# A Mamba block with a mixture of experts: one state product changes engines, a loss correction moves ahead of a projection, and ScalarE's first steps are reordered

## The reference, cut to what matters

```
h  = layernorm(layernorm(x)) @ in_proj_w.T        # 256 -> 512 channels
h  = silu(causal conv of 4 taps over time)
proj = h @ x_proj_w.T                             # 1 dt, 16 B, 16 C values per token
dt = softplus(proj[0] * dt_w + dt_b)
for every channel d and every state n of 16:
    state[t] = exp(-exp(A_log)[d,n] * dt[t,d]) * state[t-1] + B[t,n] * h[t,d]
    y[t,d]  += state[t] * C[t,n]                  # plus D[d] * h[t,d]
x1 = x + layernorm(silu(y) @ out_proj_w.T + layernorm(x))
out = x1 + layernorm(shared expert + one of 8 routed experts of layernorm(x1))
```

## Time and profile before

| | |
|---|---|
| median of three runs | 1394.33 us (1393.41 to 1395.83) |
| the profiled execution: its time / its span | 1393.79 us / 1392.0 us |
| busy of the span: PE, DVE, ACT, POOL | 86%, 77%, 57%, 75% |
| chain that ended last, by engine | PE 59%, DVE 21%, ACT 12%, issue 5% |
| scans (DVE L1126) | 256, the first at 51.0 us, the last at 969.4 us |
| mean granted TensorE clock | 0.968 of full speed |

### The profile page before, as it was taken

How to read it: one execution, slowest core, us unless ns; L and a number is a source line. 1 busy time by engine, 2 the same in 40 slices (tenths; PEclk the granted TensorE clock), 3 DMA queues, 4 the chain that set the end, 5 groups by cost and what they waited for, 6 DMA issues and landing times.

```text
span 1392.0 us, 15477 instructions
## 1 busy us (share of the span) xinstructions
PE 1194.2 (86%) x4894; PEld 535.3 (38%) x4895; DVE 1069.5 (77%) x1409; ACT 796.5 (57%) x1386; POOL 1045.7 (75%) x558
## 2 busy tenths in 40 slices
PE   5668978887996996997798798898999999999995
PEld 2222223222332432432332243243545656656663
DVE  4588899999999999899999998799241116677675
ACT  5757679779778877877967875736431111111111
POOL 0579999999999999899999999989033723554453
PEclk9889999999999999999999999999999999999998
DMA  3921210330340141042034015001278522222220
GB/s 109 277 69 60 94 61 1 122 138 0 103 157 0 63 152 46 14 140 106 1 108 137 0 63 207 20 1 55 82 270 291 180 64 73 86 79 79 84 63 15
DMA packets 72068, 127.67 MB, mean 92 GB/s; under 512 B 8759, under 2 KB 48448, under 8 KB 67904
## 3 DMA queue, kind: packets, MB, share of 16 engines
q1 hardware_dynamic: 60432, 103.72, 22.2%
q0 software_dynamic: 7152, 16.81, 3.8%
q10 hardware_dynamic: 4416, 6.29, 1.3%
HBM read 97.79 MB, written 31.76 MB: 93 GB/s over the span
## 4 chain that ended last, share of the span: by engine, by line
PE 59%; DVE 21%; ACT 12%; issue 5%; DMA 1%; DVEq 0%; POOLq 0%; POOL 0%; ACTq 0%; SPq 0%
DVE state L1126 11%; PE psX L1697 10%; PE psY L1574 10%; PE psX L1632 5%; PE bank L1531 5%; DVE bx L1114 5%; PE bank L1487 4%; ACT psX L793 3%; PE psY L1645 3%; PE bank L1714 2%; PE psY L1714 2%; PE bank L1469 2%; PE bank L1470 2%; PE bank L1471 2%; DMA xin<-in_x 1%
## 5 line engine op out<-in xcount | busy, mean ns | idle before, releaser
L517 POOL TENSOR_TENSOR state<-state,cbc 128x1024 f32<-128x1024 f32 x256 | 599.2, 2367 | 10.2 <-DVE state L1126 10.2
L1126 DVE TENSOR_TENSOR_SCAN state<-psX,bx 128x1024 f32<-128x1024 f32 x256 | 580.9, 2282 | 25.9 <-ACT psX L793 22.2
L793 ACT ACTIVATE psX<-dt,aneg 128x511 f32<-128x511 f32 x512 | 331.3, 680 | 166.4 <-DVE state L1126 166.0
L506 POOL TENSOR_TENSOR bx<-xh,bbc 128x1024 f32<-128x1024 f32 x120 | 284.8, 2374 | 89.3 <-DVE state L1126 47.1
L1574 PE MATMUL psY<-state,ident 64*64 64x512 f32 x2048 | 268.0, 617 | 0.0
L1531 PE MATMUL bank<-prow,ident 128*128 128x512 f32 x272 | 151.0, 638 | 59.4 <-DVE bx L1114 57.5
L1114 DVE TENSOR_TENSOR bx<-xh,bank 128x1024 f32<-128x1024 f32 x136 | 162.9, 1198 | 15.4 <-PE bank L1531 15.3
L998 ACT ACTIVATE sg<-psX 128x512 f32<-128x512 f32 x39 | 23.3, 597 | 196.6 <-PE psX L1697 191.4
L1574 PEld LDWEIGHTS psY<-state,ident 64*64 64x64 f32 x2048 | 61.9, 133 | 166.3 <-issue 118.4
L1531 PEld LDWEIGHTS bank<-prow,ident 128*128 128x128 f32 x272 | 44.7, 192 | 149.5 <-DVE bx L1114 107.8
L581 POOL DMA_INDIRECT ysl<-shared_rows,idx x39 | 40.3, 1034 | 80.7 <-DVE idx L1292 75.7
(11 more groups left out here) (212 smaller groups left out, 1798.2 us busy)
## 6 DMA issues: line engine op xcount, KB each, us to landing
cbc<-bc_rows SPq DMA_DIRECT2D x32, 1024.0 KB, 6.6
bbc<-bc_rows SPq DMA_DIRECT2D x16, 1024.0 KB, 6.4
slot_in<-ao SPq DMA_DIRECT2D x1, 5011.5 KB, 35.2
xsl<-slot_in SPq DMA_DIRECT2D x39, 128.5 KB
xin<-in_x SPq DMA_DIRECT2D x8, 512.0 KB, 4.1
xr<-in_x SPq DMA_DIRECT2D x8, 512.0 KB, 5.5
x_rows<-ao SPq DMA_DIRECT2D x8, 512.0 KB, 3.4
xn_rows<-xr SPq DMA_DIRECT2D x8, 512.0 KB, 3.2
```

Of the source, the lines that this page charges most:

```text
L506: nc.gpsimd.tensor_tensor(bx[q % RB][:], xh[par][:, h * CH:(h + 1) * CH], bbc[:, n // 2].unsqueeze(1).broadcast_to([P, CH, L]), ALU.mult). ...
L517: nc.gpsimd.tensor_tensor(w[:], w[:], cbc[:, n].unsqueeze(1).broadcast_to([P, CH, L]), ALU.mult).then_inc(weighted, 1)
L793: e = nc.scalar.activation(decay[q % RD][:, c, 1:L], dt[par][:, h * CH + c, 1:L], ACT.Exp, scale=aneg[:, h * CH + c, n:n + 1])
L1126: nc.vector.tensor_tensor_scan(st[q % RS][:].rearrange("p c t -> p (c t)"), decay[q % RD].rearrange("p c t -> p (c t)"), bx[q % RB][:].rea ...
```

## The change

1. `BY_POOL`: step 14 goes to GpSimd and step 12 to VectorE, instead of the other way about. Counts stay: 15 injections on GpSimd and 17 on VectorE in each iteration.
2. ScalarE: three of the squared row passes of `lead` move from q = 10 to q = 20.
3. TensorE: the first loss of each iteration (q = 19) is issued at the end of step 18, before the second projection instead of behind it.
4. `first_front` on ScalarE: the squares go to `yv` instead of `dt[0]`, so they need not wait for VectorE to have read `dt[0]`. They come earlier in the order. So does one pair of decays (step 2, taken out of iteration 0). The norm of sequence 1 comes before the last `keep_dt` and no longer waits for it.

```
-    BY_POOL = [q % 2 == 0 and q not in (14,) for q in range(Q)]
+    BY_POOL = [q % 2 == 0 and q not in (12,) for q in range(Q)]
...
-                if q == 10:
+                if q == 20:
                     for j in range(1, J):
                         row_pass(J + j, ACT.Square, mv0[par][:, j, 0:1], mv0[par][:, j, 1:2])
...
-                        if do_scan:
+                        if do_scan and (i, q) != (0, 0):
                             decays(i, par, q + RD)
...
                 def square(h, part):
-                    act.wait_ge(loss_ready if h else loss_half, 1)
-                    nc.scalar.activation(dt[0][:, part], tmp[:, part], ACT.Square,
+                    nc.scalar.activation(yv[:, part], tmp[:, part], ACT.Square,
                                          scale=HALF_ROOT).then_inc(sq_ready if h else sq_half, 1)
...
+                square(0, A)
                 relu(0, A)
-                square(0, A)
...
                 keep_dt(0)
+                square(1, B)
                 keep_dt(1)
-                relu(1, B)
-                square(1, B)
                 act.wait_ge(setup, 2)
                 decays(0, 0, 0)
+                relu(1, B)
                 decays(0, 0, 1)
                 act.wait_ge(mv0_ready, 2)
                 moments(3, 1, mv0[1], 1.0 + EPS, eps2c)
                 keep_dt(2)
+                decays(0, 0, 2)
+                apply(3, h1, xin, range(J)).then_inc(h1_ready, 1)
                 keep_dt(3)
-                act.wait_ge(dt_ready, C)
-                apply(3, h1, xin, range(J)).then_inc(h1_ready, 1)
...
                     if do_front and q in LOSS_AT:
-                        loss(i + 1, 1 - par, q)
+                        if q > LOSS_AT[0]:
+                            loss(i + 1, 1 - par, q)
...
                     elif do_back:
                         total(i - 1, 1 - par, q + Q - SUM_LAG)
+                    if do_front and q == LOSS_AT[0] - 1:
+                        loss(i + 1, 1 - par, q + 1)
                     if do_front:
                         front(i + 1, 1 - par, q)
```

More of the change, by code:

```diff
@@ L1184, in first_front @@
                     nc.vector.scalar_tensor_tensor(out=lt[:, part], in0=lt[:, part], scalar=LN_MARGIN,
-                                                   in1=dt[0][:, part], op0=ALU.add,
+                                                   in1=yv[:, part], op0=ALU.add,
                                                    op1=ALU.min).then_inc(min_done, 1)
```

## The result

| | before | changed |
|---|---|---|
| median of the first measurement, 4 runs each | 1394.76 us (1393.41 to 1395.83) | 1423.66 us (1416.99 to 1429.62) |
| ratio | | 1.0206, 95% interval 1.0149 to 1.0264 |
| the profiled execution: its time / its span | 1393.79 / 1392.0 us | 1419.02 / 1417.3 us |
| mean granted TensorE clock | 0.968 | 0.962 |
| measured again, 5 runs of the changed kernel | 1393.69 us | 1416.5 us; ratio 1.0166 (1.0152 to 1.018) |

The forecast was 1409.9 us, between 1400 and 1420. The sign holds, and so does the order of events that term 1 and term 2 describe. The size doesn't: +22.8 to +28.9 us on the medians and +25.2 in the profiled execution, where +15.6 was forecast.

What follows compares the result with a forecast made beforehand. VectorE was taken to bound half of an iteration, TensorE the end from step 25's loss. Terms 10.5 + 6.0 + 0.5 - 1.4 + 0 = +15.6 us on 1393.79, plus 0.54, gave 1409.9 us, range 1400 to 1420.

Steps and rivals of the forecast that it cites:

- term 1: Steps 10 to 14: step 12 on VectorE makes the spread for step 13 late; +1.5 us in seven iterations, +10.5.
- term 2: Step 19: minimum waits for ScalarE's square behind a later second projection; +0.7 us six times, 1.75 in iteration 0, +6.0.
- TensorE runs 3.2 to 4.2 us at half speed after this idle: First projection: TensorE idles from 436.14 to 440.95 for injection 11, then runs 3.2 to 4.2 us at half speed.
- a fixed pattern of waits, so a delay counts once: Whole program: iterations repeat the same waits, so a delay counts once for each iteration that has the stage.
- Term 3: Steps 20 to 23: squared passes moved from step 10 delay the norm VectorE's add needs; +0.5 us (0 to 1.5).
- Term 4: Last iteration, without projection: the spread of step 14 that VectorE's multiply waited behind is gone; -1.4 us (-2.5 to +1).
- Term 5: Start: earlier squares and first scan only lengthen the wait for `xin`, queued behind a 5 MB transfer; 0 us.
- VectorE passes 79.81 earlier: Iteration 0: VectorE ending its wait behind ScalarE's `xin` wait before 79.81 would show the prediction wrong.
- The waits are what they look like: Rival: injection in the gap pays -8.4 us, early loss halves the 2.90 us wait, -10; 1375 us; chance 6%.
- The clock stays down: Rival: half clock lasts to the end of the first projection, injection 13 starts at 453; +36, 1435 us; chance 5%.

Runs made afterwards that it cites:

- the matmuls of no use: The changed kernel plus four TensorE matmuls, their result overwritten, ahead of the spread of step 12: 1401.86 us, ratio 1.0058 against the kernel before.
- both parts alone: Kernel before with only steps 12 and 14 swapped between VectorE and GpSimd: 1403.14 us, 1.0063; with only the loss early: 1400.36 us, 1.004.

## Why the prediction was wrong

- **Term 1, the mechanism: right.** The spread for step 13 is late behind spread 12 and a projection that starts later. Injection 13 starts 11.71 us after scan 10 (460.33 - 448.62) instead of 9.14, 2.57 late, inside the 2.4 to 2.8 of the prediction. Scans 10 to 14 take 1.36 us more in iteration 3, where 1.2 to 1.6 was written.
- **Term 1, the size: this step failed.** The term rests on "TensorE runs 3.2 to 4.2 us at half speed after this idle". Measured from spread 12 on, it was 3.4 us in iteration 3, for which the sum came out, but 4.1 to 6.4 in the others. Scans 10 to 14 took +1.26, +2.34, +0.91, +2.34, +2.40 and +2.73 us in them, which makes 13.3 with iteration 3, not 7 x 1.5. That iteration 3 came out right is in part luck: the slow stretch was 6.8 us long, and half of it passed while TensorE was idle.
- **What could have been seen before.** The deeper error stands in the first paragraph of the prediction: "a fixed pattern of waits, so a delay counts once". The waits repeat, the clock doesn't. The kernel before shows this already. Its clock was at half for 3.4 us around the first projection in iterations 1, 3, 5 and 6, and for 6.8 us in iterations 0, 2 and 4. In those three, injection 13 already waited 1.73, 0.67 and 0.36 us for TensorE's spread. The prediction read iteration 3, one of the short kind, and the mean of all seven.
- **Not foreseen: the long iterations.** Steps 14 to 19 were counted at nothing, because VectorE has slack there. In three of seven iterations the clock fell a second time where it had not before the change, at step 17, which cost 1.1 us each there and 0.5 more at step 19: 4.9 us in all. The experiments with and without the squared passes, and with the matmuls of no use, tie it to the clock and to the parts together, not to one of them.
- **Term 2: right in six iterations** (0.69 to 0.70, or 1.18 in the long ones). In iteration 0 it was +2.65, not 1.75, since the loss waited for `dt` as well. That is also above the bound of 1.86 each time. With step 12 and the loss alone it was 4.34 there.
- **Term 3**: near enough by itself, +0.9 us by the medians and within its bound of 1.5; +1.3 in the change. Its larger price is that it comes with the long iterations, 10 us between the two kernels that differ in it.
- **Term 4: right in sign, small.** Iteration 7 gained 2.6 us, not 1.4, just outside its bound of -2.5. At the place itself, scans 12 to 14, it gained 3.1 (6.75 us instead of 9.82).
- **Term 5: the reason right.** The queue behind the zeros held `xin`, shown by moving them. The shift of 2.9 us in its issue didn't come, nor the first scan 2 us sooner. The sign "VectorE passes 79.81 earlier" was badly chosen: it passed at 81.62 in one trace of the changed kernel and at 79.39 in the other, a difference of mere scatter.
- **The rivals.** "The waits are what they look like" is refuted by both parts alone. "The clock stays down" was the near one: it named the right quantity but took it as one case for all seven iterations. In fact the slow stretch took half of the projection in three, and less of it or nothing in the others.
- **The range** had one more slow microsecond in each iteration as +3.5, but no second fall of the clock and no difference between executions.

The Trainium skill ("TensorE: Matmul & The Clock Gate", "Part 1: The HAM clock gate") says that how many matmuls run slow at a kernel's start changes from run to run, with the gate's phase at that moment. In the middle of a kernel the traces agree: three long iterations in one execution of the changed kernel, two in the other.

What is open: the four executions of the first measurement lie between 1416.99 and 1429.62 us, and no trace of one above 1419.02 exists. Their granted clock bears on it: 0.958 and 0.957 in the two executions of 1429.62 and 1428.30 us, after 0.962 and 0.961 in the other two. By an estimate from these means, some 10 to 15 us more were spent at half clock, which three or four more second falls of 3.4 us would give. That there were so many more long iterations is a guess; at about 3 us each (119.5 against 116.4) they would make the 10 us. It is not shown either why the changed kernel scattered by 12.6 us in the first measurement and by 3.0 in the second, nor why the iterations with the squared passes settle on the bad place for the clock.

## What to carry to other kernels

An idle stretch of TensorE ahead of a long group of matmuls has no fixed price. Look at the granted clock at that place in every iteration, not in one. Work out the case in which it falls when the work begins, for all iterations at once, and let the range reach there. Before an edit fills a gap on one engine, follow the row it needs on the other: here a gap of 1.2 us was filled, and a wait of 2.5 to 3.9 us opened behind it. And find the releaser of a wait before moving the other thing it waits for; where that is freed too, as with the square, look who is the bound next.

## What the runs showed of the hardware

- Four fp32 matmuls of 128x512 (eight records in the profile) took 3.70 us at full clock and 4.89 or 5.40 us where the clock was at half speed for the first part of them. The idle time ahead was the same in both cases (5.70 us ahead of spread and projection, 2.39 us ahead of the matmuls of no use).
- The granted clock was at half for 6.8 us in each of the seven iterations of the changed kernel. It fell after 2.2 to 5.2 us of the same idle time of 5.70 us.
- The parts of this change didn't add up: +9.9, +7.1, +0.9 and -0.8 us alone, +22.8 to +28.9 together.
- VectorE's `scalar_tensor_tensor` of 128x1024 with two inputs in SBUF (L1183) took 3.26 us at 48.31, with GpSimd at work for 2.2 us of it, and 1.23 us at 37.95 of the same execution, with GpSimd idle. The Trainium skill ("GPSIMD Engine Reference", "1. Specifications") says that GpSimd shares its interfaces to SBUF with VectorE, and that operations of VectorE with two inputs in SBUF contend there. The trace agrees with that at this place.
- A load of 0.5 MB landed after 4.1 us, and after 15.1, 16.7 or 18.4 us when it was issued behind 5 MB on the same queue.
